# Attention's value products in runs of four pairs, four banks for the maxima, and denominators stored octet by octet

## What is computed

```python
q, k, v = (to_tokens(q), to_tokens(k), to_tokens(v))
attn = jax.nn.softmax(jnp.einsum('bhnd,bhmd->bhnm', q, k) * scale, axis=-1)
out = jnp.einsum('bhnm,bhmd->bhnd', attn, v)
out = out.transpose(0, 1, 3, 2).reshape(B, C, H, W)
out = conv1x1(out, wo, bo)
```

## Time and profile before

| what | us |
|---|---|
| median of three runs | 5287.79 |
| profiled execution | 5287.77 |
| its span | 5285.8 |
| attention, first score to last denominator copy | 380.6 to 3899.3 |
| TensorE, VectorE, ScalarE, GpSimd busy in the span | 5059.5, 4005.8, 2791.5, 3101.3 |

### The profile page before, as it was taken

One profiled execution on the slowest core, in us unless ns is written; L12 is line 12 of the kernel. 1 busy time (PEld: TensorE's weight loads), 2 busy tenths in 40 slices (PEclk: granted clock), 3 DMA queues, 4 the chain that ended last, 5 costly groups with the idle time before them and its releaser, 6 DMA issues. The chain is left out here.

```text
span 5285.8 us, 98142 instructions
## 1 busy us (share of the span) xinstructions
PE 5059.5 (96%) x32432; PEld 2592.3 (49%) x32432; DVE 4005.8 (76%) x5144; ACT 2791.5 (53%) x5157; POOL 3101.3 (59%) x1336
## 2 busy tenths in 40 slices
PE   7989999999999999999999999999978999999797
PEld 6854444444444444444444444444436556555343
DVE  4368888888888888888888888888835878678533
ACT  2216666666666666666666666666641443443402
POOL 0008888888888888888888888888840000000000
PEclk9979999999999999999999999999989999999998
DMA  4330000010000100001000010001031000000254
GB/s 154 128 100 11 23 16 23 13 26 24 16 23 13 27 23 16 24 13 26 24 16 23 13 27 23 16 23 54 31 112 39 14 31 21 31 24 23 89 157 156
DMA packets 100938, 218.08 MB, mean 41 GB/s; under 512 B 12912, under 2 KB 22256, under 8 KB 97776
## 3 DMA queue, kind: packets, MB, share of 16 engines
q1 hardware_dynamic: 100464, 211.85, 12.8%
HBM read 131.07 MB, written 80.22 MB: 40 GB/s over the span
## 5 line engine op out<-in xcount | busy, mean ns | idle before, releaser
L757 DVE TENSOR_REDUCE b_mx<-b_pmax 128x1 f32<-128x512 f32 x4096 | 2519.3, 682 | 523.3 <-PE b_pmax L587 500.2
L723 ACT ACTIVATE b_prob<-b_pscore 128x512 f32<-128x512 f32 x4096 | 2182.7, 609 | 1251.7 <-PE b_pscore L602 1239.4
L568 POOL TENSOR_TENSOR b_sums<-b_sums,b_prob 128x1024 f32<-128x1024 f32 x1024 | 2444.2, 2387 | 460.9 <-DVE b_sums L776 319.2
L587 PE MATMUL b_pmax<-b_kst,b_qst 96*128 96x512 f32 x4096 | 1852.8, 456 | 43.7 <-DMA b_qst<-scratch_ql 15.1
L602 PE MATMUL b_pscore<-b_qst,b_kst 98*128 98x512 f32 x4096 | 1650.2, 404 | 18.9 <-ACT b_prob L723 9.7
L587 PEld LDWEIGHTS b_pmax<-b_kst,b_qst 96*128 96x128 f32 x4096 | 779.3, 190 | 1092.1 <-DVE b_mx L757 737.9
L615 PE MATMUL b_pout<-b_prob,b_vst 128*32 128x512 f32 x8192 | 999.0, 606 | 0.0
L602 PEld LDWEIGHTS b_pscore<-b_qst,b_kst 98*128 98x128 f32 x4096 | 781.7, 191 | 145.1 <-ACT b_prob L723 56.1
L562 POOL TENSOR_TENSOR b_sums<-b_prob 128x1024 f32<-128x1024 f32 x256 | 607.7, 2374 | 389.4 <-ACT b_prob L723 384.5
L1391 DVE SCALAR_TENSOR_TENSOR d_dsum<-d_ypad,d_dw,d_dsum 128x2048 f32<-128x2048 f32 x288 | 681.7, 2367 | 10.2
L776 DVE TENSOR_TENSOR b_sums<-b_prob 128x1024 f32<-128x1024 f32 x256 | 470.0, 1836 | 48.8 <-ACT b_prob L723 48.8
(11 more groups left out here) (160 smaller groups left out, 2361.1 us busy)
## 6 DMA issues: line engine op xcount, KB each, us to landing
b_kst<-scratch_kh SPq DMA_DIRECT2D x32, 512.0 KB, 9.3
b_qst<-scratch_qh SPq DMA_DIRECT2D x128, 128.0 KB, 2.5
scratch_att<-b_outn SPq DMA_DIRECT2D x128, 128.0 KB
scratch_num<-d_num SPq DMA_DIRECT2D x64, 256.0 KB, 2.0
f_num<-scratch_num SPq DMA_DIRECT2D x8, 2048.0 KB, 10.0
f_rden<-scratch_rden SPq DMA_DIRECT2D x64, 256.0 KB, 9.3
v_tok<-in_x SPq DMA_DIRECT2D x8, 1024.0 KB, 12.9
scratch_qh<-a_high SPq DMA_DIRECT2D x8, 1024.0 KB, 4.2
```

The source lines that it names most:

```text
L568: pool.tensor_tensor(acc, acc, p[:, step, :], ALU.add).then_inc(pool_added, 1)
L587: pe.matmul(pmax[max_bank(place_of(u, m))][:], qst[0:SUMS, b, t * P:(t + 1) * P], kst[0:SUMS, par, j * BANK:(j + 1) * BANK], start=True, s ...
L723: act.activation(prob[:, kt % PBUF, half * BANK:(half + 1) * BANK], pscore[score_bank(hs)][:], ACT.Exp, scale=SCALE).then_inc(exped, 1)
L757: dve.tensor_reduce(mx[:, b, t, j:j + 1], pmax[max_bank(place_of(u, m))][:], AX.X, ALU.max).then_inc(max_read, 1)
```

## The change

Six things are changed in attention, and one behind it.

1. The value products of four pairs stand in one run at an octet's end (`RUN = 4`): those of the octet before. The denominators of the octet before follow them as now.
2. The bank `b_pden` goes; the maxima have four banks. Denominators and the transposition take a bank of this ring like a maximum (`USES`, `bank_of`, `bank_free`).
3. Denominators are no longer added over the unit: each octet's are written with start and stop, copied by ScalarE at the start of the octet after next (`read_den`) and stored on their own (`store_den`); the scratch tensor is four times as large.
4. ScalarE's copies (denominators, output, values) stand in front of a key tile's exponentials; the output copy moves from tile 4 to tile 8.
5. SyncE's order in a unit is: store of octet 2 of the unit before, output store, query loads, key loads, store of octet 3, stores of octets 0 and 1 of this unit, shift rows.
6. VectorE no longer zeroes `b_pden` at the start.
7. The output stage loads eight arrays of denominators and adds them in three steps.

```diff
-    SLOTS = MAXES + 1
+    RING = 4
...
+    AHEAD = MAXES + EARLY * PER_PAIR
     T_AT = PER_PAIR
+    RUN = 4
+    OUT_AT = 2 * RUN
...
-        pmax = [pb(f"b_pmax{i}", [P, BANK]) for i in range(3)]
+        pmax = [pb(f"b_pmax{i}", [P, BANK]) for i in range(RING)]
         pout = pb("b_pout", [P, BANK])
-        pden = pb("b_pden", [P, BANK])
...
+        USES = []
+        for pair in range(PAIRS):
+            USES += [("max", PER_PAIR * pair + n, pair) for n in range(PER_PAIR - 1)]
+            if pair % (OCT // 2) == OCT // 2 - 1:
+                USES.append(("den", pair // (OCT // 2), pair))
+            USES.append(("max", PER_PAIR * pair + PER_PAIR - 1, pair))
+            if pair == PAIRS - EARLY:
+                USES.append(("turn", 0, pair))
...
+        def bank_of(c, kind, n):
+            return (c + PLACE[kind, n]) % RING
...
                     if not (first and place == 0):
-                        store(u - 1, head if c else head - 1, (c - 1) % UNITS)
+                        old = (u - 1, head if c else head - 1, (c - 1) % UNITS)
+                        store_den(*old, OCTS - 2)
+                        store(*old)
...
+                    if not (first and place == 0):
+                        store_den(*old, OCTS - 1)
+                    for o in range(OCTS - 2):
+                        store_den(u, head, c, o)
...
-                        if pair % 2:
-                            for old in (pair - 3, pair - 2):
+                        if pair % RUN == RUN - 1:
+                            for old in range(pair - 2 * RUN + 1, pair - RUN + 1):
...
-            def read_den(u):
-                act.wait_ge(den_done, done((u + 1) * OCTS))
-                act.wait_ge(den_stored, done(u * 32))
-                act.activation(outd[:], pden[:], ACT.Copy).then_inc(den_read, 1)
+            def read_den(bank, u, o):
+                act.wait_ge(den_done, done(u * OCTS + o + 1))
+                act.wait_ge(den_stored, done((u * OCTS + o) * 32))
+                act.activation(outd[:], pmax[bank][:], ACT.Copy).then_inc(den_read, 1)
...
+                        g = kt // OCT - 2
+                        if g >= 0 or behind:
+                            where = bank_of(c, "den", g + 1) if kt else bank_of((c - 1) % UNITS, "den", OCTS - 1)
+                            read_den(where, u if g >= 0 else u - 1, g % OCTS)
+                    if behind and kt == OUT_AT:
+                        read_out(u - 1)
...
-                    if behind and kt == 4:
-                        read_out(u - 1)
-                    if behind and kt == OCT + 2:
-                        read_den(u - 1)
...
-            for s in range(2):
-                sp.dma_start(dens[:, s, :], scr.att_den[:, s, :].rearrange("h (a n) -> h a n", n=BANK)).then_inc(den_in, 16)
+            for s in range(8):
+                sp.dma_start(dens[:, s, :], scr.att_den[:, s // 2, s % 2, :].rearrange(
+                    "h (a n) -> h a n", n=BANK)).then_inc(den_in, 16)
...
+            for step, half in enumerate((4, 2, 1)):
+                dve.tensor_tensor(dens[:, 0:half, :], dens[:, 0:half, :], dens[:, half:2 * half, :],
+                                  ALU.add).then_inc(chain, 1)
```

More of the change, by code:

```diff
@@ new lines, in stage_attention, with start_bank, await_read @@
+        START = [("max", m) for m in range(MAXES + T_AT)] + [("turn", 0)]
+        START += [("max", m) for m in range(MAXES + T_AT, AHEAD)]
+        def bank_of(c, kind, n):
+            return (c + PLACE[kind, n]) % RING
+        def start_bank(j):
+            return (j - len(START)) % RING
+        def await_read(eng, u, kind, n):
+            if kind == "max":
+                eng.wait_ge(max_read, maxima(AHEAD + u * MAXES + n + 1))
+            elif kind == "den":
+                eng.wait_ge(den_read, done(u * OCTS + n))
+            else:
+                eng.wait_ge(shift_low, done(u + 2))
@@ new lines, in await_start, with bank_free @@
+        def await_start(eng, j):
+            kind, n = START[j]
+            if kind == "max":
+                eng.wait_ge(max_read, maxima(n + 1))
+            else:
+                eng.wait_ge(shift_low, done(1))
+        def bank_free(eng, u, kind, n):
+            j = PLACE[kind, n] - RING
+            while True:
+                if j < 0:
+                    if is_unit(u, 0):
+                        return await_start(eng, j + len(START))
+                    u, j = u - 1, j + len(USES)
+                kind, n, pair = USES[j]
+                absent = (kind == "den" and n == 0 and is_unit(u, 0)
+                          or is_unit(u, ALL)
+                          or kind == "max" and (is_unit(u, ALL - 1) or is_unit(u, ALL - 2) and pair >= PAIRS - EARLY)
+                          or kind == "turn" and is_unit(u, ALL - 1))
+                if not absent:
+                    return await_read(eng, u, kind, n)
+                j -= RING
@@ L626, in denominators @@
                         row = (half * 2 + s) * HD
-                        mm = pe.matmul(pden[row:row + 1, :], ones[:],
+                        mm = pe.matmul(pmax[bank][row:row + 1, :], ones[:],
                                        sums[:, o % 2, s, half * BANK:(half + 1) * BANK],
-                                       start=(o == 0), stop=(o == OCTS - 1))
+                                       start=True, stop=True)
                 mm.then_inc(den_done, 1)
@@ L634, in _ @@
             pe.wait_ge(k_in[0], done(48))
[L635 to L641, removed]
+            for j, (kind, n) in enumerate(START):
+                if j == MAXES:
+                    pe.wait_ge(q_in[1], done(48))
+                if j >= RING:
+                    await_start(pe, j - RING)
+                if kind == "turn":
+                    transpose_shift(start_bank(j), 0)
+                else:
+                    max_product(start_bank(j), n % MAXES, 0, n // MAXES)
             def turn(i, first, final):
@@ L670, in turn @@
                             o = pair // (OCT // 2)
[L671 to L676, removed]
+                            if o or behind:
+                                bank_free(pe, u, "den", o)
+                                denominators(bank_of(c, "den", o), u if o else u - 1, (o - 1) % OCTS)
+                        one_maximum(3)
                         if pair == PAIRS - EARLY and not (final and place == TURN - 1):
-                            transpose_shift(u + 1)
+                            bank_free(pe, u, "turn", 0)
+                            transpose_shift(bank_of(c, "turn", 0), u + 1)
             turn(0, True, False)
@@ L683, in _ @@
             turn(TURNS - 1, False, True)
-            for pair in (PAIRS - 2, PAIRS - 1):
+            for pair in range(PAIRS - RUN, PAIRS):
                 times_v(ALL - 1, HEADS - 1, 1, UNITS - 1, pair)
-            denominators(ALL - 1, OCTS - 1)
+            bank_free(pe, ALL, "den", 0)
+            denominators(bank_of(0, "den", 0), ALL - 1, OCTS - 1)
         @block.scalar
@@ L743, in _ @@
             copy_v(0, 0)
-            high_shift(0)
+            high_shift(start_bank(MAXES + T_AT), 0)
             turn(0, True, False)
@@ L782, in _ @@
                 dve.memset(kst[SUMS:P, par, :].bitcast(F32), 1.0).then_inc(consts, 1)
[L783 to L789, removed]
+            for j, (kind, n) in enumerate(START):
+                if j == MAXES:
+                    top(0, 0)
+                if kind == "max":
+                    read_max(start_bank(j), n // MAXES, n % MAXES, n // MAXES)
+                if j == MAXES + T_AT + 1:
+                    low_shift(start_bank(MAXES + T_AT), 0)
             def turn(i, final):
@@ L805, in turn @@
                             if products:
-                                read_max(u + ahead, products[n], (place + ahead) % 2)
+                                read_max(bank_of(c, "max", PER_PAIR * pair + n), u + ahead, products[n], (place + ahead) % 2)
                             if n == 0 and pair == PAIRS - EARLY + 1 and shift:
-                                low_shift(u + 1)
+                                low_shift(bank_of(c, "turn", 0), u + 1)
             with dve.Fori(0, TURNS - 1) as i:
```

89 lines of the change are left out of this document (38 added, 51 removed).

## The result

The changed kernel takes **5297.65 us** (median of 13 runs, 5294.25 to 5303.39) against 5288.9 in its own comparison: ratio 1.0018, 95% interval 1.0010 to 1.0026. About 9 us slower, where 28 less were forecast.

The account below looks back on a forecast made before the run. TensorE (54.1 us per unit) and GpSimd (54.4) bound the kernel. TensorE's −63 − 17 + 6 + 18 = −56 was limited by GpSimd to 436.5 per turn, −36; with 8 behind the loop, −28: 5260 us, range 5246 to 5277.

Parts of the forecast that it names:

- −63: TensorE's 252 octets with maxima: each 0.25 us shorter with longer value runs and four maximum banks, 63 us less.
- −17: Transposition at a unit's end: takes a place in the ring of four banks, 63 × 0.27, 17 us less.
- +6 for the copy of values: ScalarE's once-a-head copy of values stands inside a run: 0.4 us each, 15 times, 6 us more.
- The wait for the store: ScalarE's denominator copy waits 1.9 us for octet 3's store behind key loads: 14 heads × 1.3, 18 us more, ends 0 and 30.
- upper end of 2.8: Longest wait forecast for ScalarE's denominator copy, in us: the store lands 1.7 behind the keys.
- The prediction's own sign of being wrong: TensorE's granted clock of 0.5 outside the loop's stalls would make the prediction wrong.
- Rival 3: Store behind key loads stops TensorE over 2 us and drops its clock: 5298 to 5325 us, chance 0.16.
- the last unit's clock: Last unit's 16 scores without maxima may meet a lower clock: 4 us more, range 0 to 14.
- GpSimd: right as a limit: GpSimd's chain of adds needs 13.6 us per octet, 435 per loop turn, limiting what TensorE's shorter chain can gain.
- The longer run: Value products of four pairs in one run: octet 0.25 us shorter, half the possible gain lost to VectorE's pace.
- The working with positions: Start times of a run's maxima from free pace, banks and VectorE's 0.60 us pace: position 15 starts at 7.88 us.
- Behind the loop: Output stage's extra denominator loads, 4 us more, and the last unit's possibly lower clock, 4 more: 8 us together.

## Why the prediction was wrong

- **Octets: right.** 12.96 against 13.0 forecast, with the transposition 13.81 against 13.85; the value run with denominators 4.4 against 4.45. The steps −63 and −17, with the +6 for the copy of values −74 in sum, came as −92.
- **The wait for the store: the step that failed.** Its "ends 0 and 30", taken as +18, measured +101, and the four x loads, which the sum did not price, +16. The order was seen rightly and the key loads went out 4.9 us after the octet's start (4.5 forecast). But "the keys have landed some 10 us later" was taken from the kernel before, where the last load had landed 10.6 us after the first one's issue. Here it takes 13.6 (830.75 to 844.35): the traffic falls to a share of 0.38 in 838 to 840, but 0.09 of it goes on to 844. So the keys land 18.5 us after the octet's start, not 14.2, and the store, 12 us after its issue, frees the copy 0.4 behind them: 5.7 late, over the upper end of 2.8. Why the last load takes longer than in the kernel before, no run shows. The Trainium skill (DMA: Bandwidth & Descriptors, Queues, rings and completion order) says, as the prediction cites it, that a DMA's semaphore increment lands only after every earlier write of its DMA engine. The trace agrees (0.4 us behind the last load); what was too early was the landing of the keys. And the forecast case gave the stop no price in clock: in the octet shown TensorE stood for 4.9 us and lost some 2.2 more at 0.50 behind it; over the fourteen the octet grew by 7.2, not by 1.3. The prediction's own sign of being wrong, a granted clock of 0.5 outside the loop's stalls, came.
- **Rival 3 had the mechanism** (stop, then clock) at 0.16, with 2.2 + 2.6 us per head for the 7.2 measured: the price of the clock was near, the stop too short. Its time, 5298 to 5325, lies just above the result, and that is luck: the last unit's clock did fall (0.73 from 3842 to 3898, 0.87 before in the like stretch) but cost 2 us, not 14, and the loop's turn, not priced, gave 21.
- **GpSimd: right as a limit.** The 13.6 per octet is what the run with the store first shows (13.59, 435 per turn of 32 octets), and its time is 5257.02 against 5260 forecast. In the changed kernel the stops hid it: each was time in which GpSimd caught up, so removing them gave back 40 of 117 us.
- **The longer run: missed.** The working with positions, put to four banks and runs of eight maxima, gives 12.7 per octet, less than the 13.0 for runs of sixteen. The prediction said that the long run loses half its gain, and did not compare. The runs show that it costs 94 us once GpSimd is out of the way.
- **Behind the loop: about right.** +8 forecast; +2 in the last unit and +5 behind the last denominators.

## What to carry to other kernels

A small store that a copy on the path waits for is to be issued ahead of bulk loads: behind them it landed with the last of them, and the same three loads took 10.6 us in one kernel and 13.6 in the other. The landing is to be read from a row of landings of the kernel at hand, not from where the DMA traffic falls off. When a stop is removed, ask which other chain was using it to catch up: here two limits lay one behind the other, and each alone looked worth little. Before lengthening a run to save hand-overs, compare it with the short run under the same new buffers.

## What was not expected of the hardware

At five of the loop's six turns in the changed kernel VectorE stops for 2.3 us or so, TensorE is idle for 0.2 to 1.4 us at a time, and the clock stays at 1.00. In the kernel before it fell at every turn (0.52 at the first, 0.50 at 1262 to 1264 at the second); in the changed one it fell at the first alone (0.50 from 816 to 818). The second turn after the change:

```profile
1253.87 9.06 DVE L806 TENSOR_REDUCE b_mx<-b_pmax 128x1 f32<-128x512 f32 x15 [2.30 <-PE b_pmax L630]
```

```profile
1254.00:1255.00 1.00, 0.38 (x2) 0.30 (x2) 1.00 (x2) 0.64 (x2) 0.83 (x2) 1.00 0.03 8
1255.00:1256.00 1.00, 1.00 (x5) 0.49 (x4) 1.00 (x3) 0.60 (x2) 1.00 (x1) 1.00 0.00 0
```

An added layer of denominator products costs 0.85 us with two products of 512 columns and 0.43 with four of 256 spread over all four column groups: the same columns, spread over twice the groups, take half the time, so here groups that hold one row each worked side by side and products of one group one behind the other. And the two engines that add share something: in the run with the store first, VectorE's add of 2.82 us (begun at 1999.62) ends 1.1 us into GpSimd's first add of the octet, and that add takes 3.36 us in place of 2.38. The Trainium skill (SBUF — State Buffer, SBUF: two separate sides) says that a GpSimd operation that reads SBUF and a VectorE operation with two SBUF inputs lock each other out; the trace agrees, with 1.0 us added for 1.1 of overlap.
